# Mamba-2 state space on one core: the transposes of x leave TensorE for 32x32 blocks on VectorE and 16 DMAs from ScalarE's queue

## What is computed

```
proj = layernorm(x) @ in_proj_w.T            # gate (8192), hBC (10240), dt (128 heads)
hBC  = silu(causal_conv4(hBC) + conv_b)      # x: 128 heads x 64; B, C: 8 groups x 128
x_dt = x * dt[..., None]                     # dt = softplus(dt + dt_bias)
M    = (C @ B.T) * exp(segment_sum(A * dt))  # per head, causal 128 x 128
y    = M @ x_dt + D * x
y    = rmsnorm(y) * norm_w * silu(gate)
x    = x + y @ out_proj_w.T
```

## Time and profile before

| | |
|---|---|
| median of 3 runs | 624.19 us (624.07 to 624.44) |
| the profiled execution | 624.55 us, its span in the trace 622.8 us |
| PE busy | 613.1 us, 98% |
| DVE busy | 443.0 us, 71% |
| ACT busy | 332.8 us, 53% |
| POOL busy | 224.4 us, 36% |

### The profile page before, as it was taken

One profiled execution on the slowest core, in us unless ns is written; L12 is line 12 of the kernel. 1 busy time (PEld: TensorE's weight loads), 2 busy tenths in 40 slices (PEclk: granted clock), 3 DMA queues, 4 the chain that ended last, 5 costly groups with the idle time before them and its releaser, 6 DMA issues.

```text
span 622.8 us, 11014 instructions
## 1 busy us (share of the span) xinstructions
PE 613.1 (98%) x3916; PEld 526.0 (84%) x3916; DVE 443.0 (71%) x881; ACT 332.8 (53%) x613; POOL 224.4 (36%) x169
## 2 busy tenths in 40 slices
PE   8999999999999999999999999999999999999997
PEld 7888888899999889999998889996978879787573
DVE  4533137678888888888895679789795674958773
ACT  2413115668676867686768446574634454347110
POOL 0000002269786978787876521225112021100000
PEclk9999999999999999999999999999999999999999
DMA  8600011878878788888779929285765857688400
GB/s 259 230 1 22 13 36 38 217 202 213 214 203 223 203 212 214 204 210 214 179 180 240 368 95 328 103 336 194 260 236 206 308 205 258 236 362 311 196 1 17
DMA packets 29533, 120.61 MB, mean 194 GB/s; under 512 B 7680, under 2 KB 8064, under 8 KB 21936
## 3 DMA queue, kind: packets, MB, share of 16 engines
q1 hardware_dynamic: 28912, 118.96, 61.5%
q10 hardware_dynamic: 576, 1.05, 0.6%
HBM read 86.30 MB, written 0.26 MB: 139 GB/s over the span
## 4 chain that ended last, share of the span: by engine, by line
PE 86%; DVE 6%; issue 3%; ACT 3%; DMA 1%; POOL 0%; DVEq 0%; SPq 0%; ACTq 0%
PE ps L1746 20%; PE ps L1444 12%; PE ps L1445 12%; PE ps L1446 12%; PE ps L1786 9%; PE ps L1545 4%; PE ps L1623 3%; PE ps L1775 2%; PE ps L1896 2%; DVE prob_far L1096 2%; PE ps L1505 2%; PE ps L1859 2%; DMA ring<-wk_dram 1%; PE ps L1488 1%; PE ps L1757 1%
## 5 line engine op out<-in xcount | busy, mean ns | idle before, releaser
L1746 PEld LDWEIGHTS ps<-norm_t,ring 128*128 128x128 f32 x1152 | 131.6, 192 | 4.9 <-issue 4.1
L534 POOL TENSOR_TENSOR pt_lo<-far_t,pt_hi 128x512 fp32r<-128x512 f32 (+1 forms) x94 | 112.0, 1213 | 62.3 <-ACT pt_hi L638 62.1
L1746 PE MATMUL ps<-norm_t,ring 128*128 128x128 f32 x1152 | 133.2, 276 | 0.0
L712 ACT ACTIVATE prob_far<-prob_far,neg_max 128x1024 f32<-128x1024 f32 (+2 forms) x96 | 85.5, 892 | 53.7 <-DVE neg_max L1100 53.7
L1096 DVE TENSOR_SCALAR_CACHE_REDUCE prob_far<-ps 128x256 f32<-128x256 f32 (+2 forms) x96 | 86.7, 905 | 30.2 <-PE ps L1446 29.8
L1275 DVE SCALAR_TENSOR_TENSOR acc<-raw,cw,acc 128x127 f32<-128x127 f32 (+2 forms) x240 | 83.4, 421 | 18.8 <-ACT acc L889 18.2
L1120 DVE STREAM_TRANSPOSE prob_far<-prob_far 128x2176 f32<-128x2176 f32 x30 | 73.1, 2436 | 0.8 <-ACT prob_far L712 0.2
L612 POOL TENSOR_SCALAR_AFFINE_SELECT at_hi<-a_hi 128x2048 fp32r<-128x2048 f32 x8 | 16.1, 2011 | 133.8 <-PE ps L1758 102.8
L1444 PE MATMUL ps<-k_hi,q_hi 128*128 128x512 f32 (+2 forms) x160 | 61.3, 383 | 0.7 <-DVE prob_far L1096 0.3
L1444 PE MATMUL ps<-pt_hi,v_hi 128*128 128x256 f32 x208 | 60.9, 293 | 0.6 <-POOL pt_lo L534 0.2
L1446 PE MATMUL ps<-pt_lo,v_hi 128*128 128x256 f32 x208 | 58.8, 283 | 0.0
(11 more groups left out here) (220 smaller groups left out, 1148.0 us busy)
## 6 DMA issues: line engine op xcount, KB each, us to landing
ring<-w_in_dram SPq DMA_DIRECT2D x36, 1024.0 KB, 4.9
far_t<-prob_far SPq DMA_DIRECT2D x240, 136.0 KB, 2.6
ring<-w_out_dram SPq DMA_DIRECT2D x16, 1024.0 KB, 4.9
ring<-wq_dram SPq DMA_DIRECT2D x16, 512.0 KB, 4.2
ring<-wo_dram SPq DMA_DIRECT2D x16, 512.0 KB, 3.6
w_sb<-w_dram SPq DMA_DIRECT2D x4, 896.0 KB, 9.2
ring<-ctx_t_dram SPq DMA_DIRECT2D x3, 1024.0 KB, 5.7
ring<-w_dram SPq DMA_DIRECT2D x3, 1024.0 KB, 9.1
```

The costliest lines, as they stand in the source:

```text
L534: sub = lambda dst, a, hi: pool.tensor_tensor(dst, a, hi, ALU.subtract)
L712: nc.scalar.activation(tile, tile, ACT.Exp, bias=neg_max[:, b, h:h + 1], accum_out=part_sum[:, b, h, i:i + 1]).then_inc(exp_ok, 1)
L1746: ins = mm(ps[:, bank, t * T:t * T + T], w[:, t, c, :], norm_t[:, c, :], start=(c == 0), stop=(c == NC - 1))
```

## The change

It does four things.

1. For groups 1 to 7 PE's 8 transposes go. Group 0 keeps them (`first_x_transposes`, `first_x_times_dt`).
2. DVE turns x in 32x32 blocks within each 32 partitions (`turn_x`, one instruction over 128x1024), from `xc` to a new tile `x_blk`. `xc` gets another layout, [block column, tile, 32], so that a block row is contiguous.
3. ACT's queue issues 16 DMAs (`x_moves`), each of 32 partitions by 1 KB, from `x_blk` to `x_tok`, which brings the blocks to their tokens' rows.
4. `x_times_dt` reads `x_tok` from SBUF in two instructions and not PSUM in one. `x_blk` and `x_tok` lie where `bc` lay, which group 0 alone reads.

```
+            def x_moves(g):
+                act.wait_ge(x_turned, g)
+                act.wait_ge(xdt_ok, g)
+                for i in range(4):
+                    for j in range(4):
+                        act.dma_start(x_tok[32 * j:32 * j + 32, i, :, :],
+                                      x_blk[32 * i:32 * i + 32, j, :, :]).then_inc(x_moved, 16)
...
             gate_out(step_chunk(0, 3), 1, sg[1][:, 4:8, :])
+            x_moves(1)
             squares(0)
             act.wait_ge(stack_in, 96)
             copy(c2_st[:], c2_sb[:]).then_inc(c2h_ok, 1)
...
+                if c == NC - 2:
+                    act.wait_ge(xdt_ok, GROUPS)
...
                 gate_out(step_chunk(g, 2), 0, sg[o][:, 0:4, :])
+                x_moves(g + 1)
+                gate_out(step_chunk(g, 3), 1, sg[o][:, 4:8, :])
                 if last:
                     w1_split(2)
-                gate_out(step_chunk(g, 3), 1, sg[o][:, 4:8, :])
-                if last:
                     w1_split(3)
...
+            def turn_x(g, b):
+                dve.wait_ge(silu_ok, 2 * g + 6)
+                if not (isinstance(g, int) and g == 1):
+                    dve.wait_ge(x_moved, 256 * g - 256)
+                nc.vector.transpose(x_blk[:].rearrange("p j t k -> p (j t k)"),
+                                    xc[b][:].rearrange("p j t k -> p (j t k)")).then_inc(x_turned, 1)
+
             def x_times_dt(g):
+                dve.wait_ge(x_moved, 256 * g)
+                for a in range(2):
+                    ins = nc.vector.tensor_tensor(
+                        xdt[:].rearrange("p (t a) (r c) -> p a r t c", a=2, r=2)[:, a],
+                        x_tok[:, 2 * a:2 * a + 2, :, :],
...
             def mamba_step(g, b):
                 q, k, o = 4 * g + 8, 2 * g + 6, 1 - b
-                if not (isinstance(g, int) and g == 1):
-                    x_times_dt(g)
+                x_times_dt(g)
...
                 gate(g, b)
+                turn_x(g + 1, o)
                 add_squares(g)
...
             w1_split(0)
+            x_times_dt(7)
             w1_split(1)
-            x_times_dt(7)
...
             def mamba_step(g, before_g, b, first):
-                x_transposes(g, b)
                 segments(g + 1, 1 - b, 0)
```

More of the change, by code:

```diff
@@ L239, in build @@
                 at_lo = [sbuf(st4, "at_lo0", [P, HPG, T], F32R)]
+                with ExitStack() as same_place:
+                    x_blk = sbuf(same_place, "x_blk", [P, 4, TPG, 32])
+                    x_tok = sbuf(same_place, "x_tok", [P, 4, TPG, 32])
                 bc = sbuf(st4, "bc", [P, 16, T])
@@ L268, in build @@
                 w1_sb = sbuf(st4, "w1_sb", [P, NC, FF])
+            first_x = xc[0][:].rearrange("p j t k -> p (j t k)").rearrange("p (t n) -> p t n", n=T)
             key = key_flat[:].rearrange("p (n j) -> p n j", j=BLK)
@@ L305, in build @@
                                                      sem("seg_ps"), sem("dec_ok"), sem("m_ok"))
+        x_turned, x_moved = sem("x_turned"), sem("x_moved")
         xt_ps, xdt_ok, y_ps, y_ok, ysq_ok, sq_ok = (sem("xt_ps"), sem("xdt_ok"), sem("y_ps"),
@@ L895, in conv_silu, with x_tiles, first_x_tiles, bc_tiles @@
                 act.wait_ge(taps, k + 1)
-                nc.scalar.activation(dst, acc[slot][:], ACT.Silu).then_inc(silu_ok, 1)
+                nc.scalar.activation(dst, acc[slot][:].rearrange("p t (j k) -> p t j k", k=32),
+                                     ACT.Silu).then_inc(silu_ok, 1)
+            def x_tiles(b, half):
+                return xc[b][:, :, 4 * half:4 * half + 4, :].rearrange("p j t k -> p t j k")
+            def first_x_tiles(half):
+                return first_x[:, 4 * half:4 * half + 4, :].rearrange("p t (j k) -> p t j k", k=32)
+            def bc_tiles(part):
+                return bc[:, 4 * part:4 * part + 4, :].rearrange("p t (j k) -> p t j k", k=32)
+            def x_moves(g):
[5 more added lines that the diff above has]
+                                      x_blk[32 * i:32 * i + 32, j, :, :]).then_inc(x_moved, 16)
             def gate_out(chunk, bank, dst):
@@ L916, in _ @@
             gate_out(stream(2), 0, sg[0][:, 0:4, :])
-            conv_silu(0, 0, xc[0][:, 0:4, :])
+            conv_silu(0, 0, first_x_tiles(0))
             raw_out(stream(3), 2, 0, 64, 1)
-            conv_silu(1, 1, xc[0][:, 4:8, :])
+            conv_silu(1, 1, first_x_tiles(1))
             raw_out(stream(4), 3, 1, 68, 0)
-            conv_silu(2, 0, bc[:, 0:4, :])
+            conv_silu(2, 0, bc_tiles(0))
             raw_out(stream(5), 4, 0, 72, 1)
-            conv_silu(3, 1, bc[:, 4:8, :])
+            conv_silu(3, 1, bc_tiles(1))
             raw_out(stream(6), 5, 1, 76, 0)
-            conv_silu(4, 0, bc[:, 8:12, :])
+            conv_silu(4, 0, bc_tiles(2))
             gate_out(stream(7), 1, sg[0][:, 4:8, :])
-            conv_silu(5, 1, bc[:, 12:16, :])
+            conv_silu(5, 1, bc_tiles(3))
             decay_exp(0, 0, 0)
@@ L958, in mamba_step @@
                 squares(g)
-                conv_silu(k, 0, xc[o][:, 0:4, :])
-                conv_silu(k + 1, 1, xc[o][:, 4:8, :])
+                conv_silu(k, 0, x_tiles(o, 0))
+                conv_silu(k + 1, 1, x_tiles(o, 1))
                 if last:
@@ L1297, in x_times_dt, with x_of @@
                                         ALU.mult).then_inc(xdt_ok, 1)
+            def x_of(g, b, t):
+                if isinstance(g, int) and g == 0:
+                    return first_x[:, t, :].rearrange("p (j k) -> p j k", k=32)
+                return xc[b][:, :, t, :]
             def skip_add(g, b):
@@ L1303, in skip_add @@
                     ins = nc.vector.scalar_tensor_tensor(
-                        yv[:, t, :], xc[b][:, t, :], dskip[:, bass.ds(g * TPG + t, 1)],
-                        ps[:, 4 + t // 4, (t % 4) * T:(t % 4 + 1) * T], ALU.mult, ALU.add)
+                        yv[:, t, :].rearrange("p (j k) -> p j k", k=32), x_of(g, b, t),
+                        dskip[:, bass.ds(g * TPG + t, 1)],
+                        ps[:, 4 + t // 4, (t % 4) * T:(t % 4 + 1) * T].rearrange("p (j k) -> p j k", k=32),
+                        ALU.mult, ALU.add)
                 ins.then_inc(y_ok, 1)
@@ L1329, in _ @@
                 taps_of(k + (k > 1), k, k % 2, tile)
-            x_times_dt(0)
+            first_x_times_dt(0)
             dve.wait_ge(gm_ps, 1)
@@ L1342, in _ @@
             mask_decay(1, 1, 1)
-            x_times_dt(1)
+            turn_x(1, 1)
             gate(0, 0)
@@ L1759, in segments, with first_x_transposes @@
                 ins.then_inc(seg_ps, 1)
[L1761 to L1764, removed]
+            def first_x_transposes():
+                pe.wait_ge(silu_ok, 2)
                 for t in range(TPG):
-                    ins = nc.tensor.transpose(ps[:, 4 + t // 4, (t % 4) * T:(t % 4 + 1) * T], xc[b][:, t, :], ident[:])
+                    ins = nc.tensor.transpose(ps[:, 4 + t // 4, (t % 4) * T:(t % 4 + 1) * T], first_x[:, t, :], ident[:])
                 ins.then_inc(xt_ps, 1)
@@ L1771, in y_product @@
                 pe.wait_ge(xdt_ok, g + 1)
+                if not (isinstance(g, int) and g == 0):
+                    pe.wait_ge(y_ok, g)
                 pe.wait_ge(m_ok, 2 * g + 2)
@@ L1798, in _ @@
                     segments(0, 0, 0)
-            x_transposes(0, 0)
+            first_x_transposes()
             project(0, 0)
```

14 lines of the change are left out of this document (9 added, 5 removed).

## The result

The changed kernel takes 700.13 us at the median (699.38 to 702.24), the kernel before, run beside it, 624.32 us (624.07 to 624.77): 1.1215 times as long, 95% interval 1.1198 to 1.1232. It is slower by 75.8 us where 60.7 were forecast. Its profiled execution took 700.33 us, its span is 698.6 us.

The account below looks back on a forecast made before the run. PE, busy for 98% of the span, was taken to bound the kernel. Turn by turn, +11.5, +8.9, +21.0 and +10.0 made +51.4 us, 675.6 against the median; clock loss of 10 gave 685 us, range 657 to 702.

Parts of the forecast that it names:

- T: The prediction's mark in each turn: the start on PE of `segments(g + 1, half 1)`.
- T of turn 1: First such start on PE, behind the first batch of issues: forecast 433.2 in place of 421.76, +11.5 us.
- turn 1 to turn 2: Step between these turns, where DVE's `gate` ends at T + 20.8: forecast 35.1 us in place of 26.2, +8.9.
- turns 2 to 5, each: Four steps up to turn 6: 31.3 us for 26.0 each, +21.0 together, plus 1.9 each for PE's clock.
- T of turn 6 to `skip_add(7)`: The end: last moves, landing, `x_times_dt`, then DVE's splits and sum; 36.9 us for 26.9, +10.0, plus 2.4 for the clock.
- What it removes: Seven times 0.87 us of transposes on PE, 6.1 us, giving 618.1 us at best.
- The issues on ACT and what is queued behind them: 16 issues at 0.634 us, 10.1 us, then `gate_out(g, 3)`, table load and exponential, 3.0 us, before PE's next `segments(half 1)`.
- The reason for an issue's price: Claim that an issue's time, taken as 0.634 us, goes with form (fewer than 128 partitions) and not with bytes.
- The cheap end of the range: Rival that 1 KB rows make ACT's issues cheap, 0.47 us each: 657 us, 662 with some clock loss; chance 0.13.
- The clock: PE falls to half clock behind each stop, up to 2.4 us each, together +10: 685 us, 676 if whole.
- The data branch: Moves landing 2.6 us after last issue, `x_times_dt` 1.3: `xdt` ready before `y_product` wants it, hidden by 0.7 us.
- queues held up: Rival: weight loads delay issues and landings, 0.85 us in each of seven batches and 3 us late data: 695 us; chance 0.09.

Follow-up runs that it names:

- run 1: Changed kernel without the 16 DMAs or any wait for them, `x_times_dt` reading the turned blocks where they lie: 619.33 us, 0.9923 of the kernel before.
- run 2: Changed kernel with the DMAs issued as they are, but `x_times_dt` reading `x_blk` without waiting for them: 695.13 us, 1.1126 of the kernel before.
- run 12: Changed kernel with SP's loads held as in run 11, plus 24 small matmuls on PE ahead of `segments(half 1)`: 680.88 us, 1.0911 of the kernel before.
- run 7: Changed kernel with each of the 16 DMAs over 128 partitions by 256 bytes, still from `x_blk`: 702.56 us, 1.1266 of the kernel before.
- run 10: As run 7 (128 partitions by 256 bytes), but with the 16 DMAs reading weights from HBM: 701.19 us, 1.1178 of the kernel before.
- run 11: Changed kernel with SP holding each turn's last two weight loads, and w1 and w2, until x has landed: 686.40 us, 1.0995 of the kernel before.
- run 4: Changed kernel with 48 small matmuls into an unused bank on PE ahead of `segments(half 1)`: 702.05 us, 1.1243 of the kernel before.
- run 5: Changed kernel with 24 small matmuls into an unused bank on PE ahead of `segments(half 1)`: 706.47 us, 1.1300 of the kernel before.
- run 3: Changed kernel with the same 16 DMAs issued by SP between its weight loads, none by ACT: 678.11 us, 1.0863 of the kernel before.
- run 6: Changed kernel with only 8 of the 16 DMAs, half of x used twice: 671.01 us, 1.0728 of the kernel before.
- run 9: Changed kernel moving only groups 3 to 6 by DMA, 4 issues on ACT and 12 on SP, other groups through PE: 629.85 us, 1.0097 of the kernel before.

## Why the prediction was right, and where its sizes were off

| step | predicted | measured |
|---|---|---|
| turn in blocks on DVE, `x_times_dt` | 1.15, 1.3 | 1.24, 1.29 |
| a batch of 16 issues | 10.1 (7.5 to 11.2) | 10.2 to 10.75, once 11.31 |
| T of turn 1 | 433.2 | 434.41 |
| turn 1 to turn 2 | 35.1 | 36.07 |
| turns 2 to 5, each | 31.3 + 1.9 | 33.38, 34.43, 33.65, 33.68 |
| T of turn 6 to `skip_add(7)` | 36.9 + 2.4 | 49.04 |
| `skip_add(7)` to the end of the span | unchanged, 44.0 | 43.9 |
| landing of x, median | 2.6 | 4.4 (8.95 and 7.51 at groups 6 and 7) |

**What it removes.** Right: run 1 gives 4.8 of the 6.1 us, and group 1's share is hidden by ACT's `decay`.

**The issues on ACT and what is queued behind them.** Right, and shown: the 10 us batch, six waits for `decay` (runs 1 and 2), turns of 31.65 us once clock and landings are out of the way (run 12). T is 434.41 and not 433.2 in turn 1 because the batch took 11.31 us, one of its issues being held for 1551 ns. The prediction let the batch start when `gate_out(g, 2)` had ended, T + 17.65; it starts when this copy has begun, near T + 17.1. That error of 0.6 us is hidden in turns 2 to 5 of the sum, where DVE's T + 18.15 is the later of the two.

**The reason for an issue's price.** Wrong, with the right number. "The time thus goes with the form (fewer than 128 partitions) and not with bytes" was read from a few rows in which form, engine and source changed together. Run 7 shows that partitions do not matter, and run 10, alike but for its source, that the source does: 0.623 us from SBUF, 0.454 us from HBM. Line 474, the row that seemed to speak for the form, reads from HBM and stays unexplained. The cheap end of the range (0.47 us each, 657 us) has nothing left for it: in no run did 16 issues with their source in SBUF take under 10.0 us. The rule of the Trainium skill, page "DMA: Bandwidth & Descriptors", section "Issuing engines are not separate DMA queues", that initiation is usually small relative to the DMA, does not hold for moves of this size: a 32 KB move lands 1.9 us after the start of its issue with the loads held, and its issue takes a third of that, sixteen times in a row. The 50 ns that the prediction took from the page's section on the anatomy of a DMA stand there for DMAs issued from GpSimd, so the Trainium skill does not give them for ACT's.

**The clock.** Right in kind; that the size agrees is in part luck. From T to the first issue the changed kernel takes 20.12, 20.65, 20.38 and 20.27 us in turns 2 to 5; in run 12, with a whole clock, 18.48, 18.47 and 18.46 in its turns 3 to 5. That is 7.5 us over four turns, where 4 x 1.9 = 7.6 had been forecast. But x also lands earlier in run 12. In run 11, where x lands early and only the clock is left, the same stretches give 19.01, 19.94, 20.08 and 19.17, 4.3 us in all over run 12 (with 18.47 taken for turn 2 as well). So of the 7.5 us 4.3 are shown for the clock, and the other 3.2 came back with the landings. In turns 3 to 5 of the changed kernel DVE is late by itself: `turn_x` ends at T + 20.36, 20.12 and 20.23, for T + 18.44 in run 12. In turn 5 it is DVE, and not PE at half its clock, that the batch waits for (DVE's and ACT's timelines):

```profile
590.93 1.24 DVE L1328 STREAM_TRANSPOSE x_blk<-xc 128x1024 f32<-128x1024 f32 x1
```

```profile
590.94 0.60 ACT L927 ACTIVATE sg<-ps 128x512 f32<-128x512 f32 x1 [1.79 <-PE ps L1803]
592.21 10.38 ACTq L922 DMA_DIRECT2D x_tok<-x_blk  x16
```

What a whole clock alone would be worth in the changed kernel, with its landings late, no run shows; runs 4 and 5 were to do it and did not. Run 12 against run 11 measured 5.5 us, for the part of the stops that it filled. The rule of the Trainium skill, page "TensorE: Matmul & The Clock Gate", Part 1, that an idle TensorE is put back to half its clock, agrees with these rows: up to 3.68 us for what takes 1.97, behind stops of 5.3 us and more.

**The data branch.** This is the mis-sized term. The prediction put the landing at 2.6 us, from line 377, and found `xdt` hidden by 0.7 us. The median is 4.4. In turns 2 to 5 that brings DVE's branch level with PE's (the wait of 0.25 us in turn 3). There is a second size in this branch, for which the sum has no term: the first `taps_of` of a turn, 12 instructions that took 5.35 to 5.63 us in turns 2 to 5 before, now takes 6.70. In turn 3 its first two instructions, beside POOL's `steps_a`, take 2.09 and 2.08 us and the others 0.34. The profile was to show `y_product` waiting for `xdt` for group 7 alone; it waits for groups 3 and 6 too. At group 6 the landing is 8.95 us, and `y_product` waits 4.79; at group 7 it is 7.51, 4.9 over the forecast. These two are the +9.7 us of the step from turn 6 to `skip_add(7)`. Of the whole miss of 14.4 us in the span (698.6 against 622.8 + 61.4) the step into turn 1 makes 1.2, the next 1.0, the four turns 2.5, the end 9.7. Run 11 shows the cause of the last and largest: only the timing of the loads was changed, and the step from T of turn 6 to `skip_add(7)` fell from 49.04 to 38.31 us, where 39.3 had been forecast. The rival "queues held up" had this mechanism at 0.09, but its price for late data, 3 us, was taken from landings beside SP's earlier work, and not from the loads that SP's list shows for the very moment at which groups 6 and 7 move. With 14.4 us missing, the forecast of 685 was right in its path and ACT's batch, and the range held by 1.9 us.

**What stays open.** Some 0.5 us of run 1. What sets the price of an issue beyond the source in run 10. Why single issues are held (up to 1551 ns in the changed kernel, 3022 in run 10): they come at other places in every run. Fewer and larger moves, four DMAs in place of 16, were not tried.

## What to carry to other kernels

Count the DMA issues that stand in a compute engine's list and price each like an instruction: 0.6 us here from SBUF, so 16 of them are two fifths of a 26 us turn, ahead of whatever that engine owes to others. Moving them to another engine's list saves only what that list delayed, as the last block still leaves 10 us late (run 3). And look up which large loads will be in flight when a small move must land, since its landing is not a constant: 1.9 us with the loads held, 4.4 at the median and 9.5 at worst beside them.

## What the runs showed of the hardware

- A DMA issue whose source is in SBUF takes 0.59 to 0.62 us on SP as on ACT, for 32 partitions of 1 KB and for 128 of 256 bytes (0.612 and 0.623 on ACT). The latter form takes 0.454 us on ACT with the source in HBM (run 10). SP's loads of 1 MB from HBM take 0.333 us.
- A 32 KB move lands in 1.9 us with the loads held and in up to 9.5 us (12.6 in run 7, 13.8 in run 10) beside loads of 1 MB.
- `x_times_dt`, with both operands in SBUF, takes 4.5 to 4.9 us where POOL's two `steps_a` instructions of 2.0 and 2.45 us begin just before it, 3.10 us where they begin later within it (turn 4 of run 5), and 1.29 us where they do not run beside it. The Trainium skill, page "SBUF — State Buffer", section "Who interferes with whom", says that a DVE instruction with two SBUF inputs contends with a GpSimd instruction that reads SBUF. The rows agree, and they tell whose turn it is: each of the two halves ends behind one of POOL's (in run 5 at 507.38 and 509.79 us, POOL's at 506.84 and 509.25). In this way a version with fewer or cheaper issues can lose what it wins (runs 6, 9 and 10).
- Behind a stop of 5.29 us PE's `y_product` takes 3.68 us in one turn and 2.55 in another, behind one of 0.66 us 1.97 us. The granted clock is 0.50 during the first of these, 0.75 on the mean of the second, and 1.00 during the third (from 506.1 to 508.0 us of run 12).
